# Order of SyncE's transfers at a batch's start, and new places for pieces and outputs, in an attention and expert kernel

## What is computed

```python
h = layernorm(x)                       # 16 heads of 16 channels
q, k, v = h @ Wq + bq, h @ Wk + bk, h @ Wv + bv
qc = h @ Wcq + bcq;  kc, vc = ctx @ Wck + bck, ctx @ Wcv + bcv
y = softmax(causal(q k^T / 4)) v + softmax(qc kc^T / 4) vc
x = x + y @ Wp + bp
z = layernorm(x)                       # then 8 experts of 512 tokens each (top k over all 4096)
s = (tanh(z' @ gate_w.T) + 1) / 2      # z' = z as the experts' input
o_e = (gelu(norm(z'[idx_e]) @ fc1_e.T + b1_e) @ fc2_e.T + b2_e) * s[idx_e, e]
x = x + z' + scatter_add(o_e)
```

## Time and profile before

| what | value |
|---|---|
| median of 3 runs | 1600.5 us (1596.91 to 1601.47) |
| profiled execution | 1592.22 us, its span 1590.5 us |
| TensorE busy (matmul) | 1453.4 us, 91% |
| VectorE, ScalarE, GpSimd busy | 1170.5, 902.6, 547.2 us |
| mean granted TensorE clock | 0.949 |
| attention part | from 0 to about 1293 us of the span |

### The profile page before, as it was taken

How to read it: one execution, slowest core, us unless ns; L and a number is a source line. 1 busy time by engine, 2 the same in 40 slices (tenths; PEclk the granted TensorE clock), 3 DMA queues, 4 the chain that set the end, 5 groups by cost and what they waited for, 6 DMA issues and landing times. The chain is left out here.

```text
span 1590.5 us, 25662 instructions
## 1 busy us (share of the span) xinstructions
PE 1453.4 (91%) x8560; PEld 702.0 (44%) x8560; DVE 1170.5 (74%) x3215; ACT 902.6 (57%) x1754; POOL 547.2 (34%) x1012
## 2 busy tenths in 40 slices
PE   8899999999899899989998999899989856999997
PEld 4443443444344344434443444344433323676674
DVE  6978888878788688879886988687877068455451
ACT  2177777667677677767775677567767600212211
POOL 4032333442344224432533252334113121444442
PEclk8599999999999999999998999899999977999999
DMA  6876473829373855566456736582810120345442
GB/s 176 116 128 106 89 108 103 116 67 142 101 97 87 133 113 87 101 136 106 78 118 127 101 86 110 102 113 70 124 22 3 41 84 14 94 116 122 104 110 51
DMA packets 82388, 155.22 MB, mean 98 GB/s; under 512 B 13008, under 2 KB 46416, under 8 KB 82256
## 3 DMA queue, kind: packets, MB, share of 16 engines
q1 hardware_dynamic: 74752, 142.43, 47.8%
q0 software_dynamic: 6144, 8.52, 3.2%
q10 hardware_dynamic: 1360, 2.62, 0.5%
HBM read 96.52 MB, written 53.08 MB: 94 GB/s over the span
## 5 line engine op out<-in xcount | busy, mean ns | idle before, releaser
L837 ACT ACTIVATE probs<-bank_ps 128x512 f32<-128x512 f32 (+1 forms) x1408 | 719.7, 581 | 273.7 <-PE bank_ps L628 268.9
L943 DVE TENSOR_REDUCE chunk_max<-bank_ps 128x1 f32<-128x512 f32 x1024 | 653.9, 683 | 145.5 <-PE bank_ps L667 142.0
L628 PE MATMUL bank_ps<-q_stack,k_stack 64*128 64x512 f32 (+3 forms) x1536 | 512.9, 428 | 80.0 <-ACT probs L837 49.8
L667 PE MATMUL bank_ps<-k_stack,q_stack 62*128 62x512 f32 (+3 forms) x1536 | 536.1, 438 | 9.3 <-DMA k_stack<-parts 4.8
L667 PEld LDWEIGHTS bank_ps<-k_stack,q_stack 62*128 62x128 f32 x1536 | 253.8, 194 | 357.9 <-DVE chunk_max L943 231.5
L628 PEld LDWEIGHTS bank_ps<-q_stack,k_stack 64*128 64x128 f32 x1536 | 239.7, 190 | 170.1 <-ACT probs L837 133.8
L646 PE MATMUL out_ps<-probs,v_cross 128*32 128x512 f32 x2048 | 276.4, 612 | 0.0
L946 DVE CUSTOM_DVE_ANT_0 masked<-bank_ps,causal 128x128 bf16<-128x128 f32 (+3 forms) x512 | 231.3, 483 | 43.4 <-PE bank_ps L667 40.0
L1142 POOL TENSOR_TENSOR pool_idle<-pool_idle 128x1 f32<-128x1 f32 x292 | 56.5, 193 | 526.0 <-ACT probs L837 328.0
L1475 ACT ACTIVATE h<-h_ps,b1T 128x512 f32<-128x512 f32 x64 | 44.0, 687 | 228.4 <-PE h_ps L1407 228.4
L1183 POOL TENSOR_TENSOR y_sb<-y_sb,y_add 128x256 f32<-128x256 f32 x31 | 22.7, 734 | 293.1 <-DVE y_add L1004 293.1
(11 more groups left out here) (172 smaller groups left out, 1354.4 us busy)
## 6 DMA issues: line engine op xcount, KB each, us to landing
parts_dram<-parts SPq DMA_DIRECT2D x70, 512.0 KB, 2.7
k_stack<-parts_dram SPq DMA_DIRECT2D x180, 192.0 KB, 11.7
q_stack<-parts_dram SPq DMA_DIRECT2D x180, 128.0 KB, 11.0
w1T<-in_L_ffn_fc1s SPq DMA_DIRECT2D x8, 1024.0 KB, 5.7
w2T<-in_L_ffn_fc2s SPq DMA_DIRECT2D x8, 1024.0 KB, 7.3
z_rows<-z_sb SPq DMA_DIRECT2D x8, 528.0 KB, 13.9
x_sb<-in_x SPq DMA_DIRECT2D x8, 512.0 KB, 4.3
ctxT<-in_ctx SPq DMA_DIRECT2D x8, 512.0 KB, 15.3
```

The lines of the kernel that those rows point to most:

```text
L628: mm = pe.matmul(bank_of(turn)[:, of.at:of.end], k_stack[base:base + SIDE, g, pair, of.keys:of.keys + P], q_stack[base:base + SIDE, g, pai ...
L667: return pe.matmul(bank[:, 0:n], q_stack[base:base + MAX_ROWS, g, pair, qc:qc + P], k_stack[base:base + MAX_ROWS, g, pair, k0:k0 + n], sta ...
L837: nc.scalar.activation(probs[:, buffer(u, i, p), side, columns], bank_of(("score", g, i, p, side))[:, columns], ACT.Exp, scale=SCALE)\
L943: nc.vector.tensor_reduce(dst, bank[:, 0:n], AX.X, ALU.max).then_inc(max_done, 1)
```

## The change

In SyncE's `batch`, the wait for the stores of the batch before and the load of its residual (`stored`, `load_residual`) move from the end of a batch to behind the fill of slot 3 at the start of the next; the last batch keeps them at its end too. In `PLAN` some pieces change places: `vc1` of half 1 and the `y0T` pair swap, `q` and `qc` of half 0 swap and with `kc1` and `kc0` come earlier, `proj0` goes from (1,10) to (1,7), `q` of half 1 from (2,4) to (2,2), `v`, `vc0`, `vc1` of half 0 are parted, `zT0` and `zT1` come one place or the other apart from `kc1`, and `gate` goes from (3,6) to (3,8). In `OUTPUT_PLAN` the divisions and turns are placed anew: in unit 0 `divide_self` goes from (0,5) to (0,8) and `turn_back` from (0,8) to (0,9); the other `turn_back` goes from (2,5) to (3,2).

```diff
@@ -69,18 +69,19 @@
 PROB_BUFFERS = BEHIND + 1
 
 PLAN = {
-    (0, 2): (("v", 1),), (0, 3): (("vc0", 1),), (0, 5): (("y0T0", 0), ("y0T1", 0)), (0, 6): (("vc1", 1),),
-    (0, 7): (("shift", 0),), (0, 8): (("k", 0),), (0, 9): (("qc", 0),), (1, 1): (("kc1", 0),), (1, 2): (("q", 0),),
-    (1, 4): (("kc0", 0),), (1, 7): (("shift", 0),), (1, 10): (("proj0", 0),), (2, 1): (("proj1", 0),),
-    (2, 4): (("q", 1),), (2, 5): (("v", 0), ("vc0", 0)), (2, 7): (("shift", 0),), (2, 9): (("zT0", 0),),
-    (2, 10): (("kc1", 1), ("zT1", 0)), (3, 2): (("qc", 1),), (3, 3): (("k", 1),), (3, 4): (("kc0", 1), ("vc1", 0)),
-    (3, 6): (("gate", 0),), (3, 7): (("shift", 0),),
+    (0, 2): (("v", 1),), (0, 3): (("vc0", 1),), (0, 5): (("vc1", 1),), (0, 6): (("y0T0", 0), ("y0T1", 0)),
+    (0, 7): (("shift", 0),), (0, 8): (("k", 0),), (0, 9): (("q", 0),), (0, 10): (("kc1", 0),), (1, 1): (("qc", 0),),
+    (1, 2): (("kc0", 0),), (1, 7): (("shift", 0), ("proj0", 0)), (2, 1): (("proj1", 0),), (2, 2): (("q", 1),),
+    (2, 5): (("vc0", 0),), (2, 6): (("vc1", 0),), (2, 7): (("shift", 0),), (2, 8): (("zT0", 0),),
+    (2, 10): (("zT1", 0),), (3, 0): (("kc1", 1),), (3, 2): (("qc", 1),), (3, 3): (("k", 1),), (3, 4): (("kc0", 1),),
+    (3, 6): (("v", 0),), (3, 7): (("shift", 0),), (3, 8): (("gate", 0),),
 }
 OUTPUT_PLAN = {
-    (0, 1): ("turn_cross",), (0, 3): ("divide_cross", "turn_self"), (0, 5): ("divide_self",), (0, 8): ("turn_back",),
-    (1, 0): ("turn_cross",), (1, 2): ("divide_cross", "turn_self"), (1, 4): ("divide_self",), (2, 1): ("turn_cross",),
-    (2, 3): ("divide_cross", "turn_self"), (2, 4): ("divide_self",), (2, 5): ("turn_back",), (3, 1): ("turn_cross",),
-    (3, 2): ("divide_cross", "turn_self"), (3, 4): ("divide_self",),
+    (0, 1): ("turn_cross",), (0, 2): ("divide_cross",), (0, 6): ("turn_self",), (0, 8): ("divide_self",),
+    (0, 9): ("turn_back",), (1, 0): ("turn_cross",), (1, 1): ("divide_cross",), (1, 2): ("turn_self",),
+    (1, 3): ("divide_self",), (2, 1): ("turn_cross",), (2, 2): ("divide_cross",), (2, 4): ("turn_self",),
+    (2, 5): ("divide_self",), (3, 2): ("turn_back",), (3, 4): ("turn_cross",), (3, 5): ("divide_cross", "turn_self"),
+    (3, 8): ("divide_self",),
 }
 
 
@@ -538,6 +539,9 @@
                     load_residual(b)
                 else:
                     fill(3, 2 * b + 2, N_EXP * (4 * b))
+                if b > 1:
+                    stored(b - 1)
+                    load_residual(b - 1)
                 if not last:
                     sp.wait_ge(*freed(find_piece(b, first, last, "vc1", 1)))
                     load_context(b + 1)
@@ -559,6 +563,7 @@
                     fill(2, 2 * b + 4, N_EXP * (4 * b + 3))
                 if not first:
                     store_results(b - 1, b)
+                if last:
                     stored(b)
                     load_residual(b)
 
```

## The result

The changed kernel takes 1558.0 us, median of 4 runs (1554.6 to 1562.7), against 1598.7 for the kernel before beside it: a ratio of 0.975 (95%: 0.971 to 0.9785), 41 us faster. I had forecast 1581.5, 19 faster, and a range down to 1558. The sign and the mechanism were right; the gain was twice what I gave. The step that failed is the size of the new stall (steps 3 and 4): I put it at 31.1 us, and it was 16.95.

A forecast was written before the change was run, and what follows sets the result against it. TensorE's holes for late shift rows (29.7 us) and slow clock behind them (15.9) cost 45.6; after, 23.5 + 7.6 = 31.1. Difference 14.5, with pieces 19.1: from median 1600.5 to 1581.5 us, range 1558 to 1600.

The forecast's parts named there:

- Step 3: Unit 0's outputs wait for the residual: 3.5 us stall in batches 2 to 6, 6.0 in batch 7, sum 23.5.
- Step 4: TensorE runs at slow clock behind 4 of 6 new holes, 1.9 us each: 7.6 us, bounds 0 and 11.4.
- step 1: Fill 3 goes ahead of the store wait, gate behind shift: last copy lands at 693.6 instead of 701.0 in batch 4.
- T: The start of a batch, its first exponential; 664.96 in batch 4 of the profile before.
- X: The landing of the residual's load at the start of a batch, put at 695.8 (batch 4's clock) for all six.
- Step 2: Residual queued behind fill 3 lands at 695.0, before usable at 685.85; shift rows come in time, old hole closes in full.
- Step 5: Pieces parted across iterations save 0.7 us a batch, 4.6 us in 6.5 batches; moved outputs cost nothing.
- A: Residual overtakes the fill and isn't late: all of 45.6 + 4.6 us gained, 1550 us; chance 0.10.
- B: The stall only changes its place, slow clock behind all six: new loss 48.1 us, 1598 us; chance 0.12.
- C: Fill 3 takes as long as before, residual lands at 701: 16 us slower, 1616 us; chance 0.08.
- D: Residual isn't late, but shift rows still are, behind the context: 28.6 us faster, 1572 us; chance 0.07.

The follow-up runs named there:

- e3: The changed kernel with unit 0's outputs put back where they were before, so add_heads again stands ahead of the residual: 1536.8 us, ratio to before 0.963.
- e4: The changed kernel with GpSimd's bias on the residual moved from (0,6) to (1,0), behind unit 0's outputs: 1539.2 us, ratio to before 0.964.
- e7: The changed kernel with both unit 0's outputs put back early and the residual's bias moved to (1,0): 1535.2 us, ratio to before 0.961.
- e11: The kernel before with the queue's edit, old tables kept, and the residual's bias moved to (1,0): 1555.6 us, ratio to before 0.9755.
- e10: The kernel before with only gate moved from (3,6) to (3,8), behind shift: 1583.6 us, ratio to before 0.991.
- e5: e2 with v at (3,5) and gate at (3,6), so that no piece stands behind shift: 1583.5 us, ratio to before 0.990.
- e2: The kernel before with both new tables (PLAN and OUTPUT_PLAN) and the old queue: 1561.1 us, ratio to before 0.978.
- e8: The changed kernel with the store wait and residual load moved further down SyncE's queue, behind the shift store: 1595.8 us, ratio to before 1.000.
- e6: The changed kernel with the store wait and residual load issued by GpSimd at (0,5) on its own queue: 1563.4 us, ratio to before 0.980.
- e9: The changed kernel with the store wait and residual load issued by ScalarE at (0,5) on its own queue: 1571.0 us, ratio to before 0.984.

## Why the forecast was right in kind and half in size

**What bounds it, and step 1: right.** The hole was the shift rows' and it closed. Fill 3's last copy landed at T + 28.4, 26.7, 29.5, 26.6, 28.5 and 25.8 in batches 2 to 7, forecast T + 29, before T + 35 to 38.5. In batch 4 SP issues it at T + 7.1 and the residual's load at T + 13.35, as soon as the result has landed; the timeline of SP's queue and, from the view of the DMA issues, the load's KB and us to landing:

```profile
657.23 0.45 SPq L495 DMA_DIRECT2D k_stack<-parts_dram  x1
...
663.45 0.39 SPq L531 DMA_DIRECT2D x<-in_x  x1
```

```profile
x<-in_x SPq DMA_DIRECT2D x1, 512.0 KB, 17.4
```

663.45 + 17.4 = 680.85 is T + 30.75, the X of this batch.

**Step 2: right in mechanism; the sum put the landing 1.4 us too late.** X was put at T + 30.8 in all six. It was T + 29.6, 28.8, 30.75, 27.8, 31.1 and 28.4, mean 29.4; only batches 4 and 6 are where I had them. Part of the spread is this: batches 3, 5 and 7 follow a batch that ran slowly for a stretch at its end, around `gate`. The windows of (3,8) and (3,9) in batches 1, 2, 4 and 6:

```profile
349.71:356.77 7.06, 6.95 (x56) 4.13 (x55) 6.24 (x18) 4.59 (x10) 2.90 (x9) 1.00 0.71 104
494.79:503.09 8.30, 8.30 (x56) 4.76 (x55) 6.27 (x18) 4.70 (x11) 2.89 (x9) 0.79 0.74 105
787.85:797.24 9.39, 9.39 (x55) 5.26 (x54) 6.40 (x18) 4.70 (x11) 2.90 (x9) 0.67 0.81 110
1081.47:1090.92 9.45, 9.45 (x55) 5.25 (x54) 6.40 (x18) 4.70 (x10) 2.89 (x9) 0.67 0.79 109
```

The slow stretches in batches 2, 4 and 6 put the next T off by 1.2, 2.3 and 2.4 us (against the 7.06 of batch 1) while SP's transfers run on, so batches 3, 5 and 7 issue their residual earlier against their own work (T + 12.7, 10.9 and 11.3, the others T + 13.4 to 14.1). That part of the stall is gone, and paid for at the end of the batch before. The rest isn't explained: in e3, e4 and e7, where no such stretch stands in batches 2 to 6, X still goes from T + 28.1 to T + 31.7, and its mean is 29.9, 30.0 and 29.3.

**Step 3: the step that failed in size.** I had 3.5 us in each of batches 2 to 6 and 6.0 in batch 7, 23.5, and 7.6 for the clock in step 4: 31.1. The same stretches lost 16.95 together, clock included: 1.7, 0.8, 4.2, 0 and 4.6 in batches 2 to 6, against batch 1's 14.4, and 5.65 in batch 7 (17.40 less the 11.75 of e4's window). That is 14.1 of the miss. The size hangs on X: the stall was X + 10.2 less T + 37.5, where unit 1 could start, and 2.5 more in batch 7; with the six measured X the same formula gives 14.9 instead of 23.5. That is 8.6 of the 14.1; my own range allowed 6 for X. The clock is another 2.4 (step 4), and the last 3 are half a microsecond in each batch by which the chain was shorter than I had it. VectorE's waits were 3.1, 2.2, 4.3, 1.3, 4.7 and 3.2, where I expected 4 to 5.

**Step 4: three holes slowed the clock, not four, and briefly.** TensorE's own holes of over 1.2 us there were 1.49 in batch 2, 2.64 in batch 4, 3.05 in batch 6 and 2.76 in batch 7. The granted clock fell behind the last three (0.91, 0.91 and 0.80 on the mean of the window). In batches 4 and 6 (0,10) to (1,1) is 1.35 and 1.38 longer for it, where I took 1.9; in batch 7 it is 2.5 longer than in e4. So some 5.2 us of clock where I had 7.6.

**Step 5: right in what it names, blind to the rest.** Undisturbed batches went from 144.5 to 143.4, some 7 us in 6.5 batches where I had 4.6. The account is 45.6 - 16.95 + 9.1 = 37.7, the difference in span; the 9.1 are what is left, not worked out by themselves: these 7, 1.3 in the part behind the attention (321.0 before, 319.75 after), and slow stretches elsewhere. So 4.5 of the miss of 18.6 lie here and 14.1 in steps 3 and 4. But e11 against e7 shows 20 us for the same tables once nothing waits. The 1.5 us of `gate` behind `shift` are in step 1 and yet priced only as an earlier residual. They also keep the shift rows from becoming late (e10, e5). I valued the two parts as a sum; with the queue's edit closing the old hole by itself this did no harm to the forecast of both together, but it made e2 a miss.

**The rivals.** A (residual not late) didn't hold. In e3, e4 and e7 `turn_back` doesn't wait for it; they gain 57 to 61 us where A's price was 50.2. B did not come: the new loss was 17, not 48. C is a real mechanism: e8 has it, one place further back in the queue, and with it the kernel is even with before at T + 34.7, where I had put T + 33.4; the changed kernel stands 5.3 us away from it. D: no wait for shift rows is left in the change. In e11, the same queue with the old tables, four small ones are (2.8 us).

The forecast drew rival A from the page "DMA: Bandwidth & Descriptors" of the Trainium skill, section "Queues, rings and completion order", and drew too much from it. The section says that completion isn't in order for one issuing engine, but also that a DMA engine's count on the semaphore lands only after every earlier write of that engine. By that, a load which is spread over the engines that still hold the fill can't be counted as landed ahead of it. The traces agree: in the change, e6 and e9 the residual landed behind fill 3's last copy in 18 of 18 cases.

## What to carry to other kernels

When two edits move the same chain, price the margin that each gives and not each edit's own work: here the tables alone took more than half of the hole's cost and the queue's edit all of it; what both together add is small until the next wait is gone too (41 us, then 61). A wait moved out of a queue has moved to whoever reads the last thing behind it; look in that engine's order for what stands behind the wait and can go ahead of it (here unit 0's outputs in a table, or one `if`: about 20 us). And where a stall is the small difference of two large times, give the range by the spread of the landings among batches, not by one batch.

## What the hardware showed that I had not expected

- A second queue didn't help while the first had a backlog. In e6 the load issued by GpSimd moved its first packet 9.1 to 10.6 us later, in e9 the one issued by ScalarE 6.7 to 10.2 us later, on queues of their own; then their packets ran mixed with those of SP's queue. The Trainium skill, page "DMA: Bandwidth & Descriptors", section "Queues, rings and completion order", has each DMA engine take turns among queues packet by packet. The mixed part agrees with it; for the 7 to 11 us without a packet the runs differ, and the measurement decides. That packets of the fill had already been handed on to the engines would explain it; no run here separates that.
- Holes of like length are not alike for the clock. In e2 TensorE stood for 3.1 us in batch 6 and the clock of the window stayed at 1.00; in e10 a hole of 2.2 us in batch 3 was followed by 1.2 GHz (0.75 on the mean of the window). In e6 2.5 us in batch 2 left it up and 1.7 in batch 3 didn't. These runs don't settle what tells them apart, so an estimate of clock from a hole's length carries both cases.
- The clock also falls without any hole, in the iterations around `gate`: 0.67 to 0.79 in three batches of the changed kernel, in which TensorE was busy all through (9.39 of 9.39). In e3, e4 and e7 batches 2 to 6 have no such stretch, with the same pieces at the same places.
